# Identity products around the slot marks, own rows stored after the first gather, expert rows on ScalarE, value tiles of the last tile made at the start

## The chip, the cores and the metric

The kernel runs on one core of a Trainium2 chip, in one launch. The time is the device time of that launch in microseconds (us); a smaller time is better. Of the kernel before there are three timed runs and one execution that the hardware profiler recorded.

## The reference, cut to what matters

64 images are cut into 36 patches, and each image becomes 37 rows of 192 numbers (`h`, 64 x 37 rows). Then four blocks each add to `h`: causal linear attention, a soft mixture of 64 experts, and the two that this change touches: neighborhood attention, in which each row looks at a window of 5 images by 5 rows, and a mixture of 8 experts with two experts per row.

```
# neighborhood attention (k = 5, 4 heads)
xs = gelu(convB(convA(fc1(x))) + fc1(x))
q, kmat, vmat = xs @ qkv_w.T + qkv_b
sh = clip(arange(H) - 2, 0, H - 5)          # the window is clipped at both ends
attn = softmax(q . kmat[window] + rpb)
h = h + (attn . vmat[window]) @ proj_w.T @ fc2_w.T + ...
# routed experts (E = 8, two per row, CAP = 740 places each)
logits = xf @ gate_w.T
top_p, top_i = top_k(softmax(logits), 2)
pos = place of the row among those of its expert (cumulative count)
keep = pos < cap
buf = rows put into [expert, place]
z = 2 * buf; z = z * rsqrt(mean(z * z) + 1e-6) * norm_w
g, u = split(z @ w13)
y = buf + (silu(g) * u) @ w2
out = sum over the row's two places of weight * y
```

## The kernel before

**Tiles.** The rows of three images stand in one tile of 111 partitions (`TP`), and `T` = 22 such tiles hold all of `h`, in SBUF. Each engine has its own program, written out by hand; semaphores join them. A stage is a list of steps with lags that `over_tiles` unrolls: in turn s the step with lag k works on tile s - k, in the order of the list. The first turns and the last are written out, those between are a loop.

**Neighborhood attention** (`near_pe`, `near_dve`, `near_act2`, `near_pool`). After a first part that makes the keys, TensorE does in each turn: the query of a tile (`query`, L1587), one value tile (`value`, L1593), the scores of four heads (`scores`, L1611), the projection (L1647), the transposes of the weights (L1621 and L1622), the fc2 product (L1652), and the weights times the values (L1637). POOL copies the source columns of each value tile (L1335), normalizes the softmax weights (`normalize_w`, L1346) and adds a bias to the rows (L1352), in this order within its turn. VectorE (DVE) stores values (L1431), spreads the query over heads (L1427), adds the bias to the scores and takes their maximum (L1454), copies transposed weights (L1470) and adds the result to `h` (L1477), with statistics behind it (L1479). ScalarE (ACT) takes the exponentials (L1490) and copies (L1498, L1499, L1506, L1512, L1515).

The query and the value product write the same PSUM bank 0, so `spread` waits for the value product of its turn too. A tile uses three value tiles, which `vn` holds in a ring of four. The window is clipped at the end, so the last tile (t = 21) needs three value tiles of its own, `vl`; they have the numbers 23, 24 and 25 and are made in turn 24, in a chain POOL copy, TensorE product, DVE store, each waiting for the one before.

**Routing** (`route_dve`, `route_pe`, `route_act`). DVE makes statistics, the logits and the two best experts of each row. TensorE makes the counts before each row (two products, L1668 and L1669). DVE turns them into places, and makes marks for two tiles at a time (`marks`, L1800 to L1804, 11 pairs); for each pair TensorE does four products (`slots`, L1678) that add up, for every place of every expert, the row that stands there and its weight. Meanwhile POOL makes the normalized rows `zk` (L1842, 22 instructions), SP stores them to `z_rows` in DRAM (L1874), and when the place table `take` is ready, POOL gathers the rows of expert 0 and 1 (L1852, six indirect DMAs for each expert). DVE makes `own`, the row's own part of the output, and SP stores it to the output (L1879, L1884, L1885) as soon as it is ready; POOL waits for these seven stores before its first adding store (L1865).

**Experts** (`routed_pe`): transposes of the gathered rows (L1903, L1911), gate and up products (L1929, L1934), output products (L1943), for 8 experts.

`dense_near`, which stood in the kernel before, issues products whose result nobody reads:

```
for _ in range(times):
    nc.tensor.matmul(bank[5][:, 0:256], ident, cc[:, 0:256], start=True, stop=True)
```

Of the kernel before, what the change touches and what calls it, by code (L numbers as in the profile page):

```python
# [9 lines left out]
ACT = mybir.ActivationFunctionType  # L10
# [109 lines left out]
def tower(nc, ins, rows_out):  # L120
    with ExitStack() as ctx:
# [206 lines left out]
        zs = sb("zs", [TP, T])  # L328
        rlg = sb("rlg", [TP, T, EX])
# [945 lines left out]
        def value_columns(j):  # L1275

            return j * TP if not isinstance(j, int) or j <= T else (B - WIN + PADR) * S + (j - T - 1) * TP

        def value_tiles(t):

            if isinstance(t, int):
                return [T + 1, T + 2, T + 3] if t == T - 1 else [t + 2]
            return [t + 2]
# [19 lines left out]
        def near_pool(pool):  # L1303
# [33 lines left out]
            def sources(t, q):  # L1337

                source.b = q % 2
                for j in value_tiles(t):  # L1340
                    source(j)
# [20 lines left out]
            for j in range(2):  # L1362
                source(j)
# [23 lines left out]
        def near_dve(dve):  # L1387
# [31 lines left out]
            def spread(t, q):  # L1419
# [3 lines left out]
                if after(t, 3):  # L1423
                    dve.wait_ge(s_fV, t)
# [8 lines left out]
            def values(t, q):  # L1433
                if after(t, 2):
                    dve.wait_ge(s_nA, t - 1)
                for i, j in enumerate(value_tiles(t)):
                    value(j, vl[i] if isinstance(t, int) and t == T - 1 else vn[(q + 2) % 4])
# [43 lines left out]
            over_tiles(dve, [(4, copy_w), (2, reciprocal), (1, logits), (3, values), (0, spread), (5, residual)], T, unroll=4, tail=2)  # L1481
# [40 lines left out]
        def near_pe(pe):  # L1522
# [57 lines left out]
            def query(t, q):  # L1580
                if after(t, 1):
                    pe.wait_ge(s_nq, t)
                if after(t, 4):
                    pe.wait_ge(s_fVc, t - 1)
                elif t == 0:
                    pe.wait_ge(s_fVc, 2)
                nc.tensor.matmul(bank[0][0:WN, 0:TP], Cc["wq"], xg[:, bass.ds(PADR * S + t * TP, TP)], start=True, stop=True).then_inc(s_nQ, 1)  # L1587

# [6 lines left out]
            def values(t, q):  # L1595
# [3 lines left out]
                for j in value_tiles(t):  # L1599
                    value(j, (j if isinstance(j, int) else q) % 2)  # L1600
# [24 lines left out]
            def values_out(t, q):  # L1625
# [4 lines left out]
                pe.wait_ge(s_fVc, VT if isinstance(t, int) and t == T - 1 else t + 3)  # L1630
# [27 lines left out]
        def route_act(act):  # L1658
            h_std(act, 3)
            act.wait_ge(s_ph, 9 + 2)  # L1660
            nc.scalar.activation(zrt[:], zsq[:], ACT.Sqrt, bias=eps6[:], scale=4.0).then_inc(s_hsd, 1)
            act.wait_ge(s_rt, 1)
            nc.scalar.activation(wexp[:], wdif[:], ACT.Exp).then_inc(s_re, 1)

        def route_pe(pe):
# [4 lines left out]

            def slots(p, b):

                pe.wait_ge(s_oh, p + 1)
# [6 lines left out]

            over_tiles(pe, [(0, slots)], T // 2, tail=1)

        def route_dve(dve):
# [30 lines left out]
            nc.vector.scalar_tensor_tensor(out=zs[:], in0=zs[:], scalar=2.0, in1=hrs[:], op0=ALU.mult, op1=ALU.mult).then_inc(s_ph, 1)  # L1714
# [473 lines left out]
```

## Time and profile before

| | us |
|---|---|
| three timed runs | 961.99, 970.0, 974.12 (median 970.0) |
| profiled execution | 967.93 |
| its span, first to last instruction | 965.4 |
| TensorE busy | 839.8 (87%) |
| VectorE busy | 443.0 (46%) |
| ScalarE busy | 317.8 (33%) |
| POOL busy | 306.0 (32%) |
| mean granted TensorE clock | 0.92 of full |

The span is 2.5 us shorter than the time of the same execution. A busy share is an average over stages that differ: in the experts' stage TensorE is never idle, in the routing it is idle most of the time. So the stage tells what a change in it is worth. The granted clock has two levels, 1.0 (2.4 GHz) and 0.5 (1.2 GHz), and a stretch with a figure between had both.

### The profile page before, as it was taken

What the parts mean: (1) busy time and instruction counts of PE and PEld (TensorE: products, weight loads), DVE (VectorE), ACT (ScalarE), POOL (GpSimd) and SP (SyncE); (2) the same over time, 40 slices, a digit from 0 to 9 for tenths busy, and PEclk for the clock granted to TensorE, in tenths of its full rate; (3) what the DMA queues carried; (4) which work ended last, traced back from release to release, by engine and by line L of the source; (5) the groups of instructions that cost most, each with busy time, mean ns of one, the idle gap of its engine ahead of it and who ended that gap; (6) DMA issues with size and microseconds to landing.
All of it is one profiled execution on the core that took longest, in us unless ns stands there. A gap on an engine that the chain in (4) does not pass through costs nothing.

```text
span 965.4 us, 17426 instructions
## 1 busy us (share of the span) xinstructions
PE 839.8 (87%) x6089; PEld 601.3 (62%) x6089; DVE 443.0 (46%) x1486; ACT 317.8 (33%) x906; POOL 306.0 (32%) x267
## 2 busy tenths in 40 slices
PE   6889999899999999884898899994357999999991
PEld 6778888676556665543864577773344666666661
DVE  5764655558633322222635478863871222222220
ACT  2543333226533332223033377762001212122110
POOL 1440000000000000000125254541947588888444
PEclk9999999999989999997899599996556999999996
DMA  8994000090059999995130000000224355544222
GB/s 249 259 297 187 1 2 1 1 391 2 2 204 422 421 420 421 421 380 147 43 137 0 1 2 1 0 2 1 57 78 116 81 106 105 105 93 103 39 25 24
DMA packets 59881, 129.03 MB, mean 134 GB/s; under 512 B 26334, under 2 KB 42256, under 8 KB 50112
## 3 DMA queue, kind: packets, MB, share of 16 engines
q1 hardware_dynamic: 29858, 118.72, 34.2%
q0 software_dynamic: 29952, 9.36, 7.1%
q8 instruction: 44, 0.72, 0.3%
q14 instruction: 27, 0.22, 0.1%
HBM read 115.87 MB, written 11.49 MB: 132 GB/s over the span
## 4 chain that ended last, share of the span: by engine, by line
PE 72%; DMA 12%; DVE 5%; issue 4%; ACT 2%; SPq 2%; POOL 2%; DVEq 0%; POOLq 0%; ACTq 0%
PE bank L1929 9%; PE bank L1943 6%; PE bank L1934 5%; PE bank L1213 4%; DMA w1l<-in_w_dram 4%; PE bank L1611 3%; DMA xT<-in_xT_dram 3%; PE bank L1187 3%; PE bank L849 3%; PE bank L877 3%; DMA w1s<-in_w_dram 2%; PE bank L810 2%; PE bank L1637 2%; PE bank L1191 2%; PE bank L857 2%
## 5 line engine op out<-in xcount | busy, mean ns | idle before, releaser
L1305 POOL MEMSET xg<- 96x74 f32 x1 | 0.2, 158 | 405.9 <-PE bank L1269 405.9
L1865 POOL DMA_INDIRECT out_dram<-yr,put x48 | 105.8, 2203 | 58.2 <-issue 46.8
L1929 PE MATMUL bank<-zTa,w 128*128 128x372 f32 x256 | 90.3, 497 | 0.8 <-DVE zTb L2003 0.8
L2012 DVE TENSOR_TENSOR hT<-sg,bank 128x372 f32<-128x372 f32 x64 | 31.8, 538 | 107.7 <-ACT sg L1973 66.3
L1852 POOL DMA_INDIRECT zr<-z_rows,take x48 | 66.7, 1389 | 27.1 <-issue 26.8
L1929 PEld LDWEIGHTS bank<-zTa,w 128*128 128x128 f32 x256 | 47.5, 194 | 38.2 <-ACT sg L1973 8.4
L1153 DVE COPY eh<-bank 128x384 f32<-128x384 f32 x32 | 17.9, 558 | 111.5 <-PE bank L1191 111.5
L1943 PE MATMUL bank<-w2r,hT 128*124 128x192 f32 x384 | 66.1, 329 | 0.8 <-DVE hT L2012 0.8
L1973 ACT ACTIVATE sg<-bank 128x372 f32<-128x372 f32 x64 | 27.3, 478 | 115.6 <-PE bank L1934 115.6
L1943 PEld LDWEIGHTS bank<-w2r,hT 128*124 128x124 f32 x384 | 61.9, 187 | 3.9 <-issue 3.9
L1346 POOL TENSOR_TENSOR nl<-nl,nr 111x1036 f32<-111x1036 f32 x22 | 42.1, 1914 | 60.3 <-DVE nr L1463 60.3
L1490 ACT ACTIVATE nl<-nl,nn 111x259 f32<-111x259 f32 x88 | 43.9, 501 | 40.0 <-DVE nn L1456 40.0
L1611 PE MATMUL bank<-kT,qx 96*111 (+1 forms) x176 | 52.7, 429 | 1.4 <-DVE nm L1454 1.4
L810 PE MATMUL bank<-wtok_c,xT 128*111 128x192 f32 x264 | 46.7, 331 | 8.1 <-DMA xT<-in_xT_dram 5.1
L810 PEld LDWEIGHTS bank<-wtok_c,xT 128*111 128x111 f32 x264 | 42.0, 176 | 12.8 <-issue 6.4
L1934 PE MATMUL bank<-zTb,w 64*128 64x372 f32 x256 | 48.7, 498 | 0.0
L1454 DVE CUSTOM_DVE_ANT_0 nl<-bank,bias 111x259 f32<-111x259 f32 x88 | 36.6, 424 | 15.4 <-issue 15.1
L1213 PE MATMUL bank<-w2l,eg 128*64 128x192 f32 x480 | 43.4, 330 | 0.0
L1121 ACT ACTIVATE eg<-eg 128x768 f32<-128x768 f32 x32 | 27.1, 846 | 40.6 <-DVE eg L1164 40.6
L1116 ACT COPY eh<-bank 128x384 f32<-128x384 f32 x32 | 15.4, 480 | 70.2 <-PE bank L1191 70.2
L1934 PEld LDWEIGHTS bank<-zTb,w 64*128 64x128 f32 x256 | 22.0, 186 | 24.8 <-issue 17.2
L1213 PEld LDWEIGHTS bank<-w2l,eg 128*64 128x64 f32 x480 | 32.7, 137 | 7.1 <-issue 3.3
(311 smaller groups left out, 1757.8 us busy)
## 6 DMA issues: line engine op xcount, KB each, us to landing
w1l<-in_w_dram SPq DMA_DIRECT2D x20, 1152.0 KB, 16.0
w2l<-in_w_dram SPq DMA_DIRECT2D x20, 1152.0 KB, 16.8
w1s<-in_w_dram SPq DMA_DIRECT2D x12, 1152.0 KB, 14.9
w2s<-in_w_dram SPq DMA_DIRECT2D x12, 1152.0 KB, 15.0
w<-in_w_dram SPq DMA_DIRECT2D x8, 1024.0 KB, 7.8
xt<-in_x_dram SPq DMA_DIRECT2D x22, 336.0 KB, 8.9
xT<-in_xT_dram SPq DMA_DIRECT2D x22, 333.0 KB, 8.1
w2r<-in_w2r_dram SPq DMA_DIRECT2D x8, 384.0 KB, 4.0
```

Of the source, the lines that this page charges most:

```text
L810: last = nc.tensor.matmul(bank[2 + q % 2][0:TP, 0:ED], xT[q][:, k, :], wtok_c[:, k, :], start=(k == 0), stop=(k == KC - 1))
L1213: last = nc.tensor.matmul(bank[6 + b][e * B:(e + 1) * B, 0:ED], eg[b][:, j, e, :], w2s[q][:, e, j, :], start=(j == 0), stop=(j == HB - 1))
L1346: nc.gpsimd.tensor_tensor(nl[q][:], nl[q][:], nr[b][:].unsqueeze(2).to_broadcast([TP, NHN, KW]), ALU.mult).then_inc(s_nw, 1)
L1454: nc.vector.tensor_tensor_reduce(nl[q][:, head, :], bank[1 + head % 2][0:TP, 0:KW], bias[v][:, head, :], 1.0, -3.0e38, ALU.add, ALU.max, n ...
L1490: last = nc.scalar.activation(nl[q][:, head, :], nl[q][:, head, :], ACT.Exp, bias=nn[b][:, head:head + 1], accum_out=nsum[b][:, head:head ...
L1611: nc.tensor.matmul(bank[1 + head % 2][0:TP, 0:KW], qx[q % 2][:, head, :], kT[:, bass.ds(first, KW)], start=True, stop=True).then_inc(s_nS, 1)
L1852: nc.gpsimd.indirect_dma_start(zr[b][:, j, :], None, z_rows, bass.IndirectOffsetOnAxis(ap=take[:, k:k + 1], axis=0), bounds_check=NROW - 1 ...
L1865: nc.gpsimd.indirect_dma_start(rows_out, bass.IndirectOffsetOnAxis(ap=put[:, k:k + 1], axis=0), yr[e % 2][:, j, :], None, bounds_check=OUT ...
L1929: nc.tensor.matmul(bank[to + 2 * part + half][:, 0:HS], w13[b][:, 0, at:at + 128], zTa[b][:, half * HS:(half + 1) * HS], start=True, stop= ...
L1934: nc.tensor.matmul(bank[to + 2 * part + half][:, 0:HS], w13[b][rows, 1, at:at + 128], zTb[b][rows, :], start=False, stop=True).then_inc(s_ ...
L1943: last = nc.tensor.matmul(bank[2 + j % 2][0:SP_, 0:ED], hT[:, m, j * SP_:(j + 1) * SP_], w2r[b][:, m, :], start=(m == 0), stop=(m == EH // ...
L2012: nc.vector.tensor_tensor(hT[:, m, half * HS:(half + 1) * HS], sg[half][:], bank[4 * (m % 2) + 2 + half][:, 0:HS], ALU.mult).then_inc(s_hT, 1)
```

## The change

Four edits. **Values**: the three value tiles of the last tile get the numbers 2, 3 and 4 and are made in the first three turns, each behind the query of its turn, with two identity products behind it; the ordinary value tiles move up by three numbers, and turn 24 has no value product and no POOL copy. **Identity products**: 14 after the two count products, 2 ahead of the wait of each `slots`, 22 after the last `slots`; all in bank 6. **Expert rows**: `zk` is made by ScalarE (22 activations with scale `zs` and bias `zb`, which one new DVE instruction makes) ahead of the exponential of the routing weights, and no more by POOL. **Own rows**: SP waits until the first gather (`s_zr[0]`) has landed before it stores own rows.

```
@@ value_columns, value_tiles
-            return j * TP if not isinstance(j, int) or j <= T else (B - WIN + PADR) * S + (j - T - 1) * TP
+            if isinstance(j, int) and j < 2:
+                return j * TP
+            if isinstance(j, int) and j < 5:
+                return (B - WIN + PADR) * S + (j - 2) * TP
+            return (j - 3) * TP
-            if isinstance(t, int):
-                return [T + 1, T + 2, T + 3] if t == T - 1 else [t + 2]
-            return [t + 2]
+            return [] if isinstance(t, int) and t == T - 1 else [t + 5]
@@ near_pool
-            for j in range(2):
+            for j in range(5):
                 source(j)
@@ near_dve
                 dve.wait_ge(s_nQ, t + 1)
-                if after(t, 3):
-                    dve.wait_ge(s_fV, t)
+                dve.wait_ge(s_fV, t + 3)
...
+            def last_values(t, q):
+                if isinstance(t, int) and t < 3:
+                    value(t + 2, vl[t])
...
-            over_tiles(dve, [(4, copy_w), (2, reciprocal), (1, logits), (3, values), (0, spread), (5, residual)], T, unroll=4, tail=2)
+            over_tiles(dve, [(4, copy_w), (2, reciprocal), (1, logits), (3, values), (0, spread), (0, last_values), (5, residual)], T, unroll=4, tail=2)
@@ near_pe
-                if after(t, 4):
-                    pe.wait_ge(s_fVc, t - 1)
-                elif t == 0:
-                    pe.wait_ge(s_fVc, 2)
+                pe.wait_ge(s_fVc, t + 2)
                 nc.tensor.matmul(bank[0][0:WN, 0:TP], Cc["wq"], xg[:, bass.ds(PADR * S + t * TP, TP)], start=True, stop=True).then_inc(s_nQ, 1)
+                if isinstance(t, int) and t < 3:
+                    value(t + 2, t % 2)
+                    dense_near(2)
@@ route_act
             nc.scalar.activation(zrt[:], zsq[:], ACT.Sqrt, bias=eps6[:], scale=4.0).then_inc(s_hsd, 1)
+            act.wait_ge(s_ph, 9 + 5)
+            for t in range(T):
+                nc.scalar.activation(zk[:, t, :], h[:, t, :], ACT.Identity, bias=zb[:, t:t + 1], scale=zs[:, t:t + 1]).then_inc(s_gz, 1)
             act.wait_ge(s_rt, 1)
@@ route_pe
+            def dense_route(times, to):
+                for _ in range(times):
+                    nc.tensor.matmul(bank[to][:, 0:256], ident, cc[:, 0:256], start=True, stop=True)
             def slots(p, b):
+                dense_route(2, 6)
                 pe.wait_ge(s_oh, p + 1)
...
+            dense_route(14, 6)
             over_tiles(pe, [(0, slots)], T // 2, tail=1)
+            dense_route(22, 6)
@@ route_dve
+            dve.wait_ge(s_ph, 9 + 4)
+            nc.vector.scalar_tensor_tensor(out=zb[:], in0=hmean[:], scalar=-1.0, in1=zs[:], op0=ALU.mult, op1=ALU.mult).then_inc(s_ph, 1)
@@ rows_pool
-            pool.wait_ge(s_ph, 9 + 4)
-            for t in range(T):
-                nc.gpsimd.tensor_scalar(zk[:, t, :], h[:, t, :], hmean[:, t:t + 1], zs[:, t:t + 1], ALU.subtract, ALU.mult).then_inc(s_gz, 1)
@@ routed_sp
             out_of = rows_out[0:NROW].rearrange("(t p) d -> p t d", p=TP)
+            sp.wait_ge(s_zr[0], 16 * SJ)
```

On POOL at the end of the neighborhood attention (turn 24 and behind it) stood three source copies, then the normalization of tile 21 and the bias additions:

```order
L1346 TENSOR_TENSOR nl0<-nl0,nr0 111x1036
L1352 TENSOR_TENSOR h21<-h,cc 111x192
L1335 COPY vsrc1<-xg 96x111
L1335 COPY vsrc0<-xg 96x111
L1335 COPY vsrc1<-xg 96x111
L1346 TENSOR_TENSOR nl1<-nl1,nr1 111x1036
L1352 TENSOR_TENSOR h20<-h,cc 111x192
```

The copies are gone there, and the normalization follows at once:

```order
L1338 COPY vsrc1<-xg 96x111
L1349 TENSOR_TENSOR nl0<-nl0,nr0 111x1036
L1355 TENSOR_TENSOR h21<-h,cc 111x192
L1349 TENSOR_TENSOR nl1<-nl1,nr1 111x1036
L1355 TENSOR_TENSOR h20<-h,cc 111x192
```

On TensorE at the start of the turns (`vsrc` the source of a value tile, `qx` the spread query) stood two value products, two queries, then the scores of tile 0:

```order
L1593 MATMUL bank0<-cc,vsrc0 111x96
L1593 MATMUL bank0<-cc,vsrc1 111x96
L1587 MATMUL bank0<-xg,cc 96x111 x2
L1611 MATMUL bank1<-kT,qx0 111x259
L1611 MATMUL bank2<-kT,qx0 111x259
```

Now a value product and two identity products stand behind each of the first three queries, so four identity products and two value products are ahead of the first scores:

```order
L1599 MATMUL bank0<-cc,vsrc1 111x96
L1590 MATMUL bank0<-xg,cc 96x111
L1599 MATMUL bank0<-cc,vsrc0 111x96
L1534 MATMUL bank5<-cc,identity 128x256 x2
L1590 MATMUL bank0<-xg,cc 96x111
L1599 MATMUL bank0<-cc,vsrc1 111x96
L1534 MATMUL bank5<-cc,identity 128x256 x2
L1617 MATMUL bank1<-kT,qx0 111x259
```

On TensorE in the routing stood the two count products and then the slot products of each pair (`ohc`, `ohp` the marks):

```order
L1668 MATMUL bank2<-hots,cc 111x176
L1669 MATMUL bank3<-hots,ones 111x176
L1678 MATMUL bank4<-ohc0,ohp0 124x96 x4
L1678 MATMUL bank4<-ohc1,ohp1 124x96 x4
L105 UNCONDITIONAL_BRANCH
```

Now 16 identity products (14 and the first pair's 2) lie between, two more ahead of each later pair:

```order
L1677 MATMUL bank2<-hots,cc 111x176
L1678 MATMUL bank3<-hots,ones 111x176
L1682 MATMUL bank6<-cc,identity 128x256 x16
L1692 MATMUL bank4<-ohc0,ohp0 124x96 x4
L1682 MATMUL bank6<-cc,identity 128x256 x2
L1692 MATMUL bank4<-ohc1,ohp1 124x96 x4
```

## Rows read from the trace of the kernel before

**Rows 1.** Stretches: us, busy PE, PEld, DVE, ACT, POOL, then granted clock, DMA share, GB/s
```profile
526.00:540.00 14.00, 9.96 (x34) 6.82 (x34) 4.55 (x19) 3.29 (x9) 0.77 (x3) 0.54 0.00 1
652.00:657.00 5.00, 0.61 (x10) 0.44 (x4) 1.40 (x4) 1.37 (x4) 3.65 (x5) 0.98 0.00 0
657.00:671.00 14.00, 10.78 (x76) 6.91 (x76) 3.18 (x9) 4.24 (x10) 0.52 (x1) 0.50 0.00 1
692.00:713.00 21.00, 19.79 (x88) 18.42 (x88) 15.85 (x45) 0.00 (x0) 9.55 (x7) 0.50 0.21 57
```
**Rows 2.** Timeline, last turns: start, us, engine, line, operation, [idle before <-releaser]
```profile
648.48 0.18 DVE L1463 RECIPROCAL nr<-nsum 111x4 f32<-111x4 f32 x1
...
652.75 0.52 ACT L1499 COPY pTb<-bank 37x444 f32<-37x444 f32 x1
652.78 1.91 POOL L1346 TENSOR_TENSOR nl<-nl,nr 111x1036 f32<-111x1036 f32 x1
...
656.87 0.66 PE L1593 MATMUL bank<-cc,vsrc 96*111 96x96 f32 x2 [4.39 <-DVE vl L1431]
...
658.79 0.58 PE L1621 MATMUL bank<-identity,nl 111*111 111x111 f32 x2
...
669.18 1.03 PE L1652 MATMUL bank<-cc,nz 104*111 104x208 f32 x2 [0.44 <-ACT nz L1515]
```
**Rows 3.** Timeline: queries and first scores of the first turns, and a later query
```profile
532.23 0.69 PE L1587 MATMUL bank<-xg,cc 96*96 96x111 f32 x2 [0.35 <-DVE vn L1431]
...
534.16 3.73 PE L1611 MATMUL bank<-kT,qx 96*111 96x259 f32 x8
...
539.21 0.69 PE L1587 MATMUL bank<-xg,cc 96*96 96x111 f32 x2 [1.31 <-DVE qx L1427]
...
551.34 0.36 PE L1587 MATMUL bank<-xg,cc 96*96 96x111 f32 x2
...
556.20 0.43 PE L1587 MATMUL bank<-xg,cc 96*96 96x111 f32 x2
```
**Rows 4.** Timeline: products at the full clock and at half
```profile
500.86 1.56 PE L1528 MATMUL bank<-cc,identity 128*128 128x256 f32 x6
733.82 5.18 PE L1929 MATMUL bank<-zTa,w 128*128 128x372 f32 x8 [0.80 <-DVE zTb L2003]
740.38 2.77 PE L1929 MATMUL bank<-zTa,w 128*128 128x372 f32 x8
```
**Rows 5.** Timeline: routing, from the counts to the first marks
```profile
675.57 25.98 POOL L1842 TENSOR_SCALAR zk<-h,hmean,zs 111x192 f32<-111x192 f32 x22 [12.64 <-DVE zs L1714]
675.74 0.52 DVE L1726 TENSOR_TENSOR eq<-rlg,top 111x176 f32<-111x176 f32 x1
678.27 0.33 DVE L1726 TENSOR_TENSOR eq<-lg,top 111x176 f32<-111x176 f32 x1
689.02 0.17 DVE L1784 TENSOR_SCALAR wsum<-wexp 111x22 f32<-111x22 f32 x1
691.77 3.62 PE L1678 MATMUL bank<-ohc,ohp 111*124 111x96 f32 x16 [9.58 <-DVE ohc L1804]
```
**Rows 6.** Chain of work that ended last, from the slots to expert 0
```profile
723.05 6.88 DMA zr<-z_rows,take
729.97 1.50 PE bank L1903 x6
```
**Rows 7.** Timeline: SP's stores of own rows, and POOL's first adding store
```profile
718.05 6.10 SPq L1879 DMA_DIRECT2D out_dram<-h x4
...
728.38 2.20 SPq L1885 DMA_DIRECT2D out_dram<-h x1
...
756.71 2.26 POOL L1865 DMA_INDIRECT out_dram<-yr,put x1 [12.02 <-issue]
```
**Rows 8.** The gathered rows zr: time from issue to landing, 48 transfers
```profile
DMA to landing us min/median/max: 3.9/4.3/7.2
```
**Rows 9.** Groups by line and form: an activation with a scale for each partition
```profile
L633 ACT ACTIVATE yn<-y,yrs 111x192 f32<-111x192 f32 x22 | 9.6, 441 | 0.0
```

More of the change, by code:

```diff
@@ L328, in tower @@
         zs = sb("zs", [TP, T])
+        zb = sb("zb", [TP, T])
         rlg = sb("rlg", [TP, T, EX])
@@ L1337, in sources @@
             def sources(t, q):
-                source.b = q % 2
+                source.b = (q + 1) % 2
                 for j in value_tiles(t):
@@ L1435, in values @@
                     dve.wait_ge(s_nA, t - 1)
-                for i, j in enumerate(value_tiles(t)):
-                    value(j, vl[i] if isinstance(t, int) and t == T - 1 else vn[(q + 2) % 4])
+                for j in value_tiles(t):
+                    value(j, vn[(q + 2) % 4])
+            def last_values(t, q):
+                if isinstance(t, int) and t < 3:
+                    value(t + 2, vl[t])
             for j in range(2):
@@ L1599, in values @@
                 for j in value_tiles(t):
-                    value(j, (j if isinstance(j, int) else q) % 2)
+                    value(j, (q + 1) % 2)
             for j in range(2):
@@ L1629, in values_out @@
                 tiles = vl if isinstance(t, int) and t == T - 1 else [vn[(q + i) % 4] for i in range(3)]
-                pe.wait_ge(s_fVc, VT if isinstance(t, int) and t == T - 1 else t + 3)
+                pe.wait_ge(s_fVc, VT if isinstance(t, int) and t == T - 1 else t + 6)
                 if after(t, 1):
```

## The prediction

> **What bounds the kernel now.** I read the busy time by stretch first, then the timeline and the chain that ended last where a stretch looks poor. Up to the first turns of the neighborhood attention and from expert 0's products on, nothing is changed, so only some 200 us between can move. In them TensorE runs long at the lower clock, 0.50: in most of 526 to 540, in all of 657 to 671 and of 692 to 713 [rows 1]. Three waits stand out.
>
> The first is at the end of the neighborhood attention. From 652.5 to 656.9 TensorE does nothing and its clock has gone to 0.50 when it goes on [rows 1, 2]. The weights of tile 21 could be normalized from 648.66 on, when the reciprocal is done, but POOL begins at 652.78 [rows 2], since the source copies of the last tile's values stand ahead of it and each waits for a product on TensorE. POOL's bias additions come after, DVE's residual waits for these, and DVE's stores of values stand behind the residual, so TensorE waits for them.
>
> The second is the routing: TensorE is idle for 9.6 us ahead of the first slot product, and then does the 44 slot products at half clock, 0.45 us each (3.62 us for 8) [rows 5], with DVE waiting for it in turn.
>
> The third is the gather. The sixth indirect DMA of expert 0 is issued at 723.05 and lands 6.88 us later, at 729.97, when the transposes start [rows 6]; the least of the 48 is 3.9 and the median 4.3 us [rows 8]. SP's stores of own rows, 718.05 to 730.6, lie beside it [rows 7].
>
> **Last turns.** Without the three copies the normalization starts at 648.7 and ends at 650.6, and nothing late is left ahead of the bias additions. The next to be late is ScalarE's copy of transposed weights, which ends at 653.27; the transposes of tile 21 can start at 653.35 instead of 658.79 [rows 2]: 5.4 us. From there to the end of the last fc2 product at 670.21 it was 11.4 us. I estimate that hand-offs over ScalarE take 4.2 of it and TensorE 7.2, at half clock. If the clock stays high this is halved, 3.6 us less, as the gate products took 5.18 us at half and 2.77 at the full clock [rows 4]. So the bounds are -5.4 (clock falls at once) and -9.0 (it stays). The stall that had let it fall is gone, but these turns have no scores and TensorE will still wait a microsecond at each hand-off. I take -8.0.
>
> **First turns.** The three value products are now here, with six identity products. The identity products at full clock: 6 records, 3 products, in 1.56 us with the last one's latency, so 0.47 us each from start to start; at half clock I scale by columns from the gate product, 5.18 us for 4 products of 372 columns [rows 4], to 0.86 us. The first scores began at 534.16 [rows 3]. Now ahead of them, from 532.23 on at half clock: query and value product (1.0), two identity products (1.7), again both (2.7), so they begin at about 537.9, 3.7 us late. Against that TensorE now works without a gap from 532.2 on, and the clock should rise in or before these scores instead of in the turn before 551.34. Scores that took 3.73 us then take about 2.5, and a turn from query to query 4.9 (551.34 to 556.20), where the two turns from 539.21 to 551.34 took 6.1 each [rows 3]. Laid out: scores from 537.9 to 540.4, then 0.9 for DVE's last maximum and spread as before (537.9 to 539.2 with its wait), third query at 541.3 (was 539.21); then two turns of 4.9, the first with 0.9 of identity products, so the fifth query at 551.9 (was 551.34). That is +0.5. Bounds: -1.5 if the clock rises at once, +4.5 if not before the third turn. The later turns have the same order and the same waits as before, with other numbers.
>
> **ScalarE's rows.** The nearest row is an activation of 111x192 with a scale for each partition, 0.441 us [rows 9]; 22 of them are 9.7 us, from about 675.8 to 685.5. Behind them stands the exponential of the routing weights, with a table load of some 1.3 us, so it is done at about 687; DVE reads it at 689.02 [rows 5]. That cover is 2 us; without it each microsecond would be paid. SP stores `zk` long before the gathers. DVE has one more instruction with a semaphore wait ahead of the first maximum: +0.2. POOL's 25.98 us go away [rows 5], and they were hidden; but the same comparison on DVE took 0.52 us as POOL's first one began and 0.33 later, also beside POOL [rows 5]. I take -0.4 for all of DVE's chain.
>
> **Routing.** The count products end at 682.2, 9.58 us before the first slot product at 691.77 [rows 5]. The 14 identity products are 12.0 us if the clock stays at half. The first gate products, from 733.82 on without a pause, took 5.18 us for eight records, those from 740.38 on 2.77 [rows 4]: the clock rose after some 5 us of unbroken work. With 5 us at half (6 products) and 8 at 0.47, they end at 691.0, and the pair of the first slots at 691.9: +0.2. Then a pair of tiles costs 2 x 0.47 of identity products and 4 x 0.24 of slot products (0.45 scaled by 2.77/5.18), 1.9 us, against 1.81 before (3.62 / 2). DVE's marks are shorter: it is busy for 15.85 of the 21 us [rows 1], about 1.5 a pair, so TensorE sets the pace. The first four products and ten such pairs are 19.9 us; before it was 20.4 (691.77 to the end of the 44th at 712.2, of which 0.5 in waits). With the +0.2 I take -0.3. The higher clock is spent on the products that keep it. Bounds -2.5 (identity products hidden better) and +2.
>
> **Gather.** `take` is ready, and POOL issues, at the same distance from the last slot product. Without SP's stores beside them the rows land in 3.9 to 4.3 us instead of 6.88 [rows 6, 8]: -2.8, bounds 0 and -3.0. The stores took 12.5 us before [rows 7]; begun at 727 they end at about 740 on the scale of the trace before. POOL waits for them ahead of its gather for expert 2, 10 us of issue, and the first adding store, at 756.71 before [rows 7], would be due some 3 us earlier: hidden with 3 us to spare. Later stores would delay the first adding stores, which only expert 2's output buffers wait for.
>
> **First expert.** The 22 identity products last 10.4 us, the wait from the last slot product to the landed rows about 15. The idle 4.7 us are as long as the 4.4 us after which the clock was at half [rows 1, 2]. So the gate products start cold, as before: 0. If the clock were kept, the first 5.18 us would be 2.77, the transposes 1.3 us less: -3.9 in all [rows 4].
>
> **Sum.** -8.0 + 0.5 + 0.2 - 0.4 - 0.3 - 2.8 = -10.8. Against the profiled execution's own 967.9 (span 965.4 and 2.5 around it) that is 957.1. This execution was 2 us below the median of 970.0, which itself has runs from 962 to 974; I forecast 957.
>
> **Rivals.**
> A, the forecast, clock as above: 957, chance 0.47, own range 951 to 962.
> B, the clock is kept throughout: -9.0 in the last turns, -1.5 in the first, -2.5 in the routing, -3.0 for the gather, -3.9 for the first expert, -0.2 for DVE; -20.1 together, 948. For it: in rows from 740 on the clock stays high. Against it: the idle 4.7 us. Chance 0.20.
> C, the first turns lose and the last ones run cold: -5.4 + 4.5 - 0.2 + 0 - 2.8 = -4, 964. For it: from 534 to 551 TensorE was busy most of the time and stayed at half, with waits for DVE of 1.3 us [rows 3]. Or the stores were not what delayed the gather (that term at 0): 960. Chance 0.23.
> D, slower: the identity products don't raise the clock in the routing. For it: 692 to 713 had TensorE busy for 19.79 of 21 us, still at 0.50 [rows 1]. Then a pair costs 1.7 + 1.8 us; 14 products make the first slots 4 us late, ten pairs with 1.7 more each 17 more, and the 22 end 18.9 us after the last slot, 3.7 us after the rows. 4 + 17 + 3.7 - 2.8 = 22; with -8.0 for the last turns, +0.5 for the first and -0.2 for DVE's chain +14, 982. It decides once the clock is still low after the fourth pair, since 4 + 4 x 1.7 then eat up the 10.5 won elsewhere. Against it: the gate products, issued without a wait, raised the clock [rows 4], and the 14 identity products come without a wait too. Chance 0.05.
> E, POOL had held DVE up throughout: if each of its instructions in front of 691.77, 14 of the 22, cost DVE the 0.19 us between the two comparisons [rows 5], 2.6 us go instead of 0.4: 955. Against it: the second comparison also ran beside POOL, unhindered. Chance 0.05. The Trainium skill, "SBUF — State Buffer", section "Who interferes with whom", has a DVE instruction with two SBUF inputs and a GpSimd instruction that reads SBUF exclude each other for a whole instruction, which speaks for E; the row of the second comparison does not show it.
> That the change doesn't do what it says would be to have POOL's normalization still late; the order excludes it.
>
> **Range and chances.** A with its range, E, C up to 964 and a part of B hold 8 in 10 between 948 and 965. Faster by over 2% (below 950.7 against the median, 948.5 against the profiled time) is most of B and a little of A: 0.17. Slower by over 2% is a worse D: 0.02. Within 2%, about what a measurement of this kernel can tell from no change, the rest, 0.81.
>
> **What would show it.** Right: no idle time of over 1.5 us on TensorE between the loop's end and the last fc2 product, statistics some 8 us earlier; granted clock near 1.0 among the slot products; a landing of about 4 us; half clock in the first gate products. Wrong: a third query later than 543, DVE waiting for ScalarE's exponential, slots at 0.50, POOL waiting for own rows ahead of its first adding store.

## The result, and the profile after

The changed kernel takes 955.3 us (median of 20 runs, 951.2 to 963.2), the kernel before 968.0 us in the same series (20 runs, 962.0 to 974.1). The ratio is 0.989, with a 95% interval of 0.9867 to 0.9913: about 10.7 us less (8.4 to 12.9 by the interval; the two medians are 12.7 apart). So the gain is clear of the noise and under 2%. The profiled execution of the changed kernel has a span of 949.4 us, the one of before 965.4. One run of this study, of 958.8 us in f1 below, is over 1.5% above the fastest run of its kernel and counts as slow, and f1's figures leave it out.

Of these 16.0 us, 5.1 are not the change's. They lie ahead of the first query of the neighborhood attention, in code that no edit touches: the first query starts at 532.23 us before and at 527.14 after, and in the fourteen profiled executions of this study it starts anywhere from 523.9 to 537.0. So everything below is counted from the first query on. From there to the end it is 433.2 us before and 422.3 after, 10.9 less, which agrees with the ratio. (f0, the same kernel in another execution, has 423.0, 10.2 less.)

The table cuts this stretch at rows that every kernel here has, and gives each piece in us. "Marks" is the slot stage, from the first slot product to the moment when VectorE, which waits for the last one, reads the sums. "All" is their sum, and "time" that of the whole profiled execution, which has the varying part ahead of the first query in it too. "To counts" ends where the first count product starts, "to transposes" where the first product on the gathered rows of expert 0 starts. f0 is the changed kernel profiled once more. Each row is one execution, and where kernels have the same code a stage can still differ: the last turns by 1.5 us (23.63 to 25.18), the stage to the end by 1.7 (234.35 to 236.08 with 22 identity products ahead of it).

| | first to sixth query | to last query | to last fc2 product's end | to counts | to first slot product | marks | to transposes | to the end | all | time |
|---|---|---|---|---|---|---|---|---|---|---|
| before | 23.97 | 81.43 | 32.58 | 10.46 | 11.10 | 20.44 | 17.76 | 235.43 | 433.2 | 967.9 |
| after | 25.74 | 82.03 | 25.17 | 10.36 | 10.01 | 18.49 | 14.96 | 235.50 | 422.3 | 951.2 |
| e1 | 24.06 | 81.40 | 32.58 | 10.35 | 10.00 | 18.49 | 15.01 | 235.15 | 427.0 | 960.4 |
| e2 | 26.29 | 82.03 | 23.92 | 10.34 | 10.34 | 18.39 | 14.93 | 236.08 | 422.3 | 948.0 |
| e3 | 25.34 | 82.03 | 23.75 | 10.36 | 10.56 | 18.39 | 17.97 | 234.37 | 422.8 | 954.7 |
| e4 | 25.38 | 82.02 | 23.75 | 10.34 | 10.58 | 18.39 | 14.87 | 232.08 | 417.4 | 947.1 |
| e5 | 25.42 | 82.02 | 23.63 | 10.44 | 11.08 | 18.49 | 14.96 | 235.65 | 421.7 | 956.7 |
| e6 | 25.37 | 82.02 | 23.69 | 10.36 | 10.01 | 20.15 | 15.09 | 235.40 | 422.1 | 960.9 |
| e7 | 25.01 | 82.03 | 23.93 | 10.36 | 10.01 | 18.33 | 15.13 | 235.89 | 420.7 | 954.2 |
| e8 | 25.80 | 82.03 | 25.18 | 10.36 | 10.89 | 27.02 | 14.91 | 234.35 | 430.5 | 967.6 |
| f0 | 27.54 | 82.02 | 23.91 | 10.36 | 10.13 | 18.39 | 15.06 | 235.60 | 423.0 | 953.9 |
| f1 | 28.02 | 82.03 | 23.92 | 10.35 | 10.01 | 15.08 | 14.99 | 233.57 | 418.0 | 949.6 |
| f2 | 24.26 | 82.03 | 23.68 | 10.34 | 11.58 | 14.98 | 14.87 | 231.66 | 413.4 | 950.3 |
| g1 | 23.64 | 82.02 | 23.69 | 10.35 | 9.35 | 15.09 | 15.05 | 233.71 | 412.9 | 944.7 |

The first view of after is the busy time by stretch, with the columns of [rows 1]: us, busy PE, PEld, DVE, ACT, POOL, then granted clock, DMA share, GB/s.

```profile
649.00:654.00 5.00, 3.78 (x54) 2.57 (x50) 2.09 (x5) 2.42 (x8) 1.05 (x2) 1.00 0.01 3
654.00:661.00 7.00, 4.21 (x31) 2.06 (x30) 1.52 (x5) 3.17 (x7) 0.00 (x0) 0.56 0.00 0
671.00:681.00 10.00, 10.00 (x41) 8.47 (x40) 8.31 (x35) 5.83 (x12) 0.00 (x0) 0.78 0.61 166
681.00:700.00 19.00, 19.00 (x132) 17.82 (x131) 15.03 (x46) 0.00 (x0) 0.00 (x0) 1.00 0.00 1
714.00:718.00 4.00, 3.16 (x19) 2.41 (x20) 1.21 (x2) 1.85 (x2) 3.26 (x3) 0.50 0.79 209
```

The marks, at 0.50 before [rows 1], now run at 1.00 (681 to 700). The last turns begin at 1.00 and end at about half; expert 0 still starts at 0.50 (714 to 718).

The timeline of TensorE over the last turns (start, us, engine, line, operation, idle before and releaser) answers to [rows 2]:

```profile
650.65 0.42 PE L1627 MATMUL bank<-identity,nl 111*111 111x111 f32 x2 [0.44 <-issue]
...
655.10 1.03 PE L1658 MATMUL bank<-cc,nz 104*111 104x208 f32 x2 [1.07 <-ACT nz L1521]
...
659.05 1.03 PE L1658 MATMUL bank<-cc,nz 104*111 104x208 f32 x2 [0.44 <-ACT nz L1521]
```

The stop of 4.39 us is gone; the longest wait left is 1.07 us. Behind it an fc2 product takes 1.03 us where it took 0.52 a turn earlier: there the clock fell.

The same view over the routing, to set beside [rows 5], then the gather:

```profile
670.44 0.93 PE L1677 MATMUL bank<-hots,cc 111*111 111x176 f32 x2 [10.35 <-DVE hots L1760]
...
671.74 8.85 PE L1682 MATMUL bank<-cc,identity 128*128 128x256 f32 x32
680.45 1.11 PE L1692 MATMUL bank<-ohc,ohp 111*124 111x96 f32 x8
681.39 1.06 PE L1682 MATMUL bank<-cc,identity 128*128 128x256 f32 x4
...
683.12 1.05 PE L1682 MATMUL bank<-cc,identity 128*128 128x256 f32 x4
...
698.74 9.69 PE L1682 MATMUL bank<-cc,identity 128*128 128x256 f32 x44
713.90 1.50 PE L1918 MATMUL bank<-identity,zr 124*128 124x124 f32 x6 [5.47 <-DMA zr<-z_rows,take]
```

A product is two records, so the slot products of a pair are x8. From 681.39 to 683.12 a pair and its two identity products take 1.73 us. And the chain of work that ended last, at the gather, beside [rows 6]:

```profile
708.07 1.38 POOL zr L1866
709.75 4.10 DMA zr<-z_rows,take
713.90 1.50 PE bank L1918 x6
```

The rows that held the kernel up land 4.10 us after their issue, not 6.88.

### The profile page after: what moved, and what is told of

It reads as the page before. It is cut to its first block, busy times and chain, and to the rows that moved or that the text cites. A ratio compares the mean times of both kernels' runs of the same rounds, so it can differ in the third digit from the quotient of the medians.

```text
span 949.4 us, 17704 instructions
## 1 busy us (share of the span) xinstructions
PE 849.1 (89%) x6217; PEld 612.3 (64%) x6217; DVE 441.2 (46%) x1487; ACT 327.1 (34%) x928; POOL 279.8 (29%) x245
## 4 chain that ended last, share of the span: by engine, by line
PE 73%; DMA 12%; issue 4%; DVE 3%; SPq 3%; ACT 2%; POOL 1%; DVEq 0%; POOLq 0%; ACTq 0%
PE bank L1944 9%; PE bank L1958 6%; PE bank L1949 5%; DMA w1s<-in_w_dram 4%; PE bank L1617 4%; PE bank L1214 4%; PE bank L850 3%; PE bank L1188 3%; PE bank L811 3%; PE bank L878 3%; DMA xT<-in_xT_dram 3%; DMA w2l<-eo 2%; DMA w1l<-in_w_dram 2%; PE bank L1682 2%; PE bank L1627 2%
## 5 line engine op out<-in xcount | busy, mean ns | idle before, releaser
L1617 PE MATMUL bank<-kT,qx 96*111 (+1 forms) x176 | 49.6, 406 | 2.2 <-DVE nm L1460 2.0
```

The source lines that it names most:

```text
L1617: nc.tensor.matmul(bank[1 + head % 2][0:TP, 0:KW], qx[q % 2][:, head, :], kT[:, bass.ds(first, KW)], start=True, stop=True).then_inc(s_nS, 1)
```

## The experiments

Each experiment is the changed kernel with the edit shown. e1 to e8 were each executed once, with a profile; f0, f1, f2 and g1 were also timed six times, in rounds with the kernel before. The table above has the stages of all of them.

**e1: value tiles of the last tile late again.** Numbering, rings and waits of the value tiles as in the kernel before, and so none of the six identity products of the first turns either; the other three edits stay. One piece of the edit:

```
-            return [] if isinstance(t, int) and t == T - 1 else [t + 5]
+            if isinstance(t, int):
+                return [T + 1, T + 2, T + 3] if t == T - 1 else [t + 2]
+            return [t + 2]
```

> The changed kernel with the last tile's three value tiles back in turn 24, without the identity products of the first turns; the routing as changed. In the trace of the changed kernel the stretch from the last query to the end of the last fc2 product is 25.2 us, in that of before 32.6. Theory (POOL's source copies hold back the normalization of tile 21, and the clock falls in the stall): it is 32 to 33 us again, and the stretch from the first query to the sixth is 24.0 again, not 25.7; in all 5 to 6 us slower than the changed kernel. Rival (part of the 7.4 us came from the clock's phase in that one execution): 27 to 30 us.

The last turns take 32.58 us again, to a hundredth what they took before, and the first ones 24.06. So the edit is worth -7.4 there in the profiled execution of after and costs +1.7 in the first turns. In all e1 is 4.7 us slower than after, where 5 to 6 were expected. The loop between takes 81.40 with the old numbering and 82.0 with the new one, in every kernel: 0.6 us that the prediction did not have. POOL's timeline of e1 has the mechanism as the prediction named it:

```profile
647.83 0.28 POOL L1336 COPY vsrc<-xg 96x111 f32<-96x111 f32 x1 [2.15 <-PE bank L1594]
651.94 0.28 POOL L1336 COPY vsrc<-xg 96x111 f32<-96x111 f32 x1 [3.83 <-PE bank L1594]
652.18 1.91 POOL L1347 TENSOR_TENSOR nl<-nl,nr 111x1036 f32<-111x1036 f32 x1
```

The normalization (L1347) follows the third copy, which waits 3.83 us for TensorE.

**e2: no identity products in the first turns.**

```
                     value(t + 2, t % 2)
-                    dense_near(2)
```

> The changed kernel without the six identity products of the first three turns; the value tiles stay there. Theory of the prediction (the products cost 3.5 us ahead of the first scores and give it back by an earlier clock): first query to first scores 2 to 2.5 us instead of 5.0, first to sixth query 24 to 26 us, within 1 us of the changed kernel's 25.7. Rival (they only cost): under 23 us, since the waits of DVE set the pace of these turns. Rival 2 (they pay): over 27 us, half clock up to the sixth query.

26.29 us to the sixth query: 0.3 above what the theory allowed, far from the first rival (under 23) and below the second (over 27), so none of the three is met. The first scores come 2.92 us after the first query and run at half clock (3.76 us for eight records), as the next two groups do. Kernels that have the products there in the changed kernel's form were profiled nine times: seven of them need 25.0 to 25.8, two (f0 and f1) 27.5 and 28.0. So the value tiles alone cost 2.3 us, and beside this one profile the six identity products give back 0.5 to 1.3 or lose 1.2 to 1.7; with one profile without them, what they are worth on the whole is not settled. What sets which it is, the timelines of TensorE show. After:

```profile
530.45 1.81 PE L1534 MATMUL bank<-cc,identity 128*128 128x256 f32 x4
532.11 1.04 PE L1617 MATMUL bank<-kT,qx 96*111 96x259 f32 x4
...
536.00 0.40 PE L1590 MATMUL bank<-xg,cc 96*96 96x111 f32 x2 [1.58 <-DVE vl L1433]
...
541.25 0.41 PE L1590 MATMUL bank<-xg,cc 96*96 96x111 f32 x2 [1.61 <-DVE vl L1433]
...
541.67 3.58 PE L1617 MATMUL bank<-kT,qx 96*111 96x259 f32 x8
```

and f0, the same kernel:

```profile
532.50 1.97 PE L1534 MATMUL bank<-cc,identity 128*128 128x256 f32 x4
534.26 1.32 PE L1617 MATMUL bank<-kT,qx 96*111 96x259 f32 x4
...
538.45 0.66 PE L1590 MATMUL bank<-xg,cc 96*96 96x111 f32 x2 [1.58 <-DVE vl L1433]
...
545.26 0.66 PE L1590 MATMUL bank<-xg,cc 96*96 96x111 f32 x2 [1.60 <-DVE vl L1433]
```

In both the clock rises near the end of the identity products. In f0 it is some tenths later (1.97 and 1.32 us against 1.81 and 1.04), and after the first wait of 1.58 us for VectorE it is at half again (a query takes 0.66 us, not 0.40); in after it falls only behind the second such wait. The turns with the waits then take 6.8 and 6.7 us, or 5.25 and 6.0.

**e3: own rows stored at once**, ahead of the gather, as before.

```
             out_of = rows_out[0:NROW].rearrange("(t p) d -> p t d", p=TP)
-            sp.wait_ge(s_zr[0], 16 * SJ)
```

> The changed kernel with SP storing own rows at once, beside the first gather. Theory (SP's stores delay the gathered rows): the sixth transfer of expert 0 lands 6.5 to 7 us after its issue instead of 4.1, the first transposes start 17.5 to 17.8 us after the last slot product instead of 15.0; 2.5 to 3 us slower. Rival (the landing of 6.88 was a matter of that execution, or came with POOL's earlier work): 15 us and no change.

The wait for the rows is 17.97 us instead of 14.96. The other stages differ from after's by up to 1.4 us in both directions, but each stays within what the kernels without this edit show. In e3's chain the landing stands as

```profile
711.38 7.10 DMA zr<-z_rows,take
```

So the stores beside it were what delayed it, by 3.0 us (a landing of 6.5 to 7 us had been expected).

**e4: 34 identity products behind the marks** instead of 22.

```
-            dense_route(22, 6)
+            dense_route(34, 6)
```

> The changed kernel with 34 identity products behind the last slot product instead of 22, so that they last until the rows of expert 0 land. In the changed kernel TensorE is idle for 5.5 us there, the clock is at half in the transposes and the first gate products. Theory (these 5.5 us let the clock fall; the 22 products give nothing): from the landing to the second group of gate products 6.7 us instead of 10.6, so 3.5 to 4 us faster. Rival (transposes and their hand-offs let the clock fall anyway): 9 to 10.6 us, no change.

Its timeline of TensorE:

```profile
698.05 14.87 PE L1682 MATMUL bank<-cc,identity 128*128 128x256 f32 x68
713.12 0.85 PE L1918 MATMUL bank<-identity,zr 124*128 124x124 f32 x6 [0.20 <-DMA zr<-z_rows,take]
714.32 0.85 PE L1926 MATMUL bank<-identity,zr 124*64 124x124 f32 x12 [0.34 <-ACT zTa L1980]
715.98 2.74 PE L1944 MATMUL bank<-zTa,w 128*128 128x372 f32 x8 [0.80 <-DVE zTb L2018]
```

The transposes take 0.85 instead of 1.50 us, the first gate products 2.74 instead of 5.30: from the landing to the end of these gate products 3.6 us less, and from the transposes to the end of the kernel 3.4. The changed kernel stops its identity products 5.47 us too early for this. Both figures depend on the execution, for with 22 products the first gate products take anything from 4.17 (e8) to 5.30 us; beside e8 the gain would be 2.3 us.

**e5: expert rows on POOL again.**

```
-            act.wait_ge(s_ph, 9 + 5)
-            for t in range(T):
-                nc.scalar.activation(zk[:, t, :], h[:, t, :], ACT.Identity, bias=zb[:, t:t + 1], scale=zs[:, t:t + 1]).then_inc(s_gz, 1)
+            pool.wait_ge(s_ph, 9 + 4)
+            for t in range(T):
+                nc.gpsimd.tensor_scalar(zk[:, t, :], h[:, t, :], hmean[:, t:t + 1], zs[:, t:t + 1], ALU.subtract, ALU.mult).then_inc(s_gz, 1)
```

> The changed kernel with the 22 normalized expert rows made by POOL again, after DVE's scale, and no bias instruction. In the changed kernel the stretch from the end of the last fc2 product to the first slot product is 20.4 to 20.9 us, in that of before 21.6; and the slot stage 18.4 to 18.5 us. Theory E of the prediction (POOL's instructions hold up DVE): 21.4 to 21.7 us, and the first pairs of marks slower. Rival (the 1.2 us came from something else, such as the clock or the counts): 20.4 to 20.9 us.

From the counts to the first slot product 11.08 us, where the changed kernel has 10.01 and the kernel before has 11.10. That stretch is VectorE's here: TensorE has done its identity products and waits 0.28 us for the marks. From the end of the count products it is 9.57 us in e5 and 9.58 before, with POOL's instructions, and 8.50 in after, e6 and g1, without them. The marks behind it take 18.49 us as in after: the slower first pairs that the theory added did not come. VectorE's timeline in e5, with POOL beside it:

```profile
669.80 0.52 DVE L1739 TENSOR_TENSOR eq<-rlg,top 111x176 f32<-111x176 f32 x1
...
676.64 0.34 DVE L1768 COPY sums<-sums 111x8 f32<-111x8 f32 x1
```

and in the changed kernel:

```profile
665.83 0.34 DVE L1744 TENSOR_TENSOR eq<-rlg,top 111x176 f32<-111x176 f32 x1
...
672.36 0.17 DVE L1773 COPY sums<-sums 111x8 f32<-111x8 f32 x1
```

POOL's instructions of 1.18 us each (25.98 / 22 [rows 5]) cost VectorE 0.1 to 0.25 us now and then, most often in the short copies behind the counts, and add up to 1.1 us. The Trainium skill, "SBUF — State Buffer", section "Who interferes with whom", names a VectorE instruction with two SBUF inputs and, in the 2-port modes, a copy as those that contend with GpSimd, and says of the port pair that they share: "Whoever issues first gets the shared pair for the whole instruction". The rows agree that they interfere (the comparison has two SBUF inputs), and not on the size: no instruction of VectorE was held up by anything like POOL's 1.18 us.

**e6: no identity products in the routing at all** (neither the 14, nor the 2 per pair, nor the 22).

> The changed kernel without any identity product in the routing (the 14, the 2 in each pair, the 22). Theory (the slot products without them run at half clock, 0.45 us each, 1.81 us a pair, and TensorE sets the pace): the slot stage 20.2 to 20.5 us instead of 18.4; nothing else moves, so 2 us slower. Rival (the slot stage became shorter since POOL no longer works beside DVE): 18.4 to 19 us.

The marks take 20.15 us, as they did before (20.44). The busy time by stretch:

```profile
688.00:699.00 11.00, 10.48 (x48) 10.00 (x48) 8.84 (x25) 0.00 (x0) 0.00 (x0) 0.50 0.00 0
699.00:708.00 9.00, 8.96 (x41) 8.34 (x40) 6.29 (x18) 0.00 (x0) 0.00 (x0) 0.50 0.00 0
```

TensorE is busy for 19.44 of 20 us and stays at 0.50. All 58 identity products of the routing together are worth 1.7 us. The counts to the first slot product are 10.01 us here as in after: VectorE sets that stretch, and in after the 14 products just fit into it. They don't always. In e2, e3, e4 and f0 TensorE goes from the identity products to the slot products without a gap, and the first slot product comes after 10.13 to 10.58 us (10.89 in e8, with two more ahead of it): where the clock rises late, the products hold it up by 0.1 to 0.6 us.

**e7 and e8: none, or four, ahead of each pair** instead of two; the 14 and the 22 stay.

> The changed kernel with the 14 and the 22 identity products, but none between the pairs of slot products. Theory 1 (the clock that the 14 raised stays up, since TensorE then waits for DVE's marks only a part of each pair): pairs at DVE's pace of 1.65 us, the stage 17 to 17.6 us instead of 18.4, so the two in each pair cost 1 us. Theory 2 (the waits for DVE let the clock fall in the stage): 19.5 to 20.5 us.

> The changed kernel with four identity products ahead of each pair instead of two. Theory (TensorE sets the pace of the slot stage, and a pair costs what its products cost at the full clock): two more at 0.44 us each, a pair 2.62 instead of 1.74 us, the stage 27 to 28 us instead of 18.4. Rival (DVE's marks set the pace): under 20 us.

e7 needs 18.33 us for the marks, as with two: between the two theories (17 to 17.6, and 19.5 to 20.5), since the pace that the first had for VectorE was too slow and the fall of the clock, which the second has, came late. Its timeline and its stretches:

```profile
683.05 1.11 PE L1691 MATMUL bank<-ohc,ohp 111*124 111x96 f32 x8 [0.42 <-DVE ohc L1821]
...
688.64 12.71 PE L1691 MATMUL bank<-ohc,ohp 111*124 111x96 f32 x56 [0.29 <-DVE ohc L1821]
```

```profile
682.00:689.00 7.00, 5.42 (x37) 4.33 (x37) 7.00 (x21) 0.00 (x0) 0.00 (x0) 0.98 0.00 0
689.00:699.00 10.00, 9.94 (x47) 9.46 (x47) 8.07 (x23) 0.00 (x0) 0.00 (x0) 0.50 0.00 0
```

For five pairs VectorE sets the pace, 1.40 us a pair (four from 683.05 to 688.64), and TensorE waits 0.29 us in each. Then the clock falls, TensorE sets the pace at half clock, 1.8 us a pair, and never gets it back. With two identity products (after) the clock stays, but they cost TensorE 0.89 us a pair, so 1.73 is what a pair takes. The two come out even. With four, a pair takes 2.60 us (690.36 to 692.96) and the stage 27.02:

```profile
690.36 1.92 PE L1682 MATMUL bank<-cc,identity 128*128 128x256 f32 x8
692.12 1.01 PE L1692 MATMUL bank<-ohc,ohp 111*124 111x96 f32 x8
692.96 1.92 PE L1682 MATMUL bank<-cc,identity 128*128 128x256 f32 x8
```

That pointed to one: 0.44 + 0.84 = 1.28 us for TensorE, less than VectorE's 1.40, with 0.12 to wait instead of 0.29.

**f0, f1, f2: the changed kernel, one ahead of each pair, and more in other places.** f1 has one identity product per pair and 34 behind the marks. f2 adds to f1:

```
@@ query
+                if isinstance(t, int) and t in (2, 3):
+                    dense_near(3)
@@ fc2 of the last two tiles (dense_last: the same product in bank 2)
+                if isinstance(t, int) and t >= NLT:
+                    dense_last(2)
@@ route_pe, ahead of the counts and behind them
+            for _ in range(12):
+                nc.tensor.matmul(bank[2][:, 0:256], ident, cc[:, 0:256], start=True, stop=True)
...
-            dense_route(14, 6)
+            dense_route(18, 6)
```

> The changed kernel once more, so that f1 and f2 have it beside them on the same chip. Nothing is altered. From the two executions timed side by side so far: 0.989 of the kernel before, interval about 0.985 to 0.993, so 955 to 958 us beside 967. Stages as in its first profile: last query to last fc2 product 23.8 to 25.2 us, counts to first slot product 10.0 to 10.6, slot stage 18.4 to 18.5, gather 15.0.

> The changed kernel with one identity product instead of two ahead of each pair of marks, and 34 instead of 22 behind the last slot product. Theory (the identity products are worth what the clock they keep gives back, and no more of them is wanted than keeps it): a pair of slots then costs TensorE 0.44 + 0.84 = 1.28 us, less than VectorE's 1.40, so VectorE sets the pace and the slot stage takes 15 to 16 us instead of 18.4, at granted clock 1.00; behind it the 34 products keep the clock up to the transposes, 3.4 us less as in e4. Together 6 to 7 us less than the changed kernel, some 949 to 951 where that has 956. Rival: with 0.12 us of waiting in each pair the clock falls among the slots, as it did with none in e7, and the stage stays at 18 to 19 us; then only e4's 3.4 us are left, some 952 to 953.

> f1 with identity products in three more places where TensorE waits at half clock: three ahead of the third and fourth query of the first turns, two ahead of each fc2 product of the last two tiles, twelve ahead of the count products and 18 instead of 14 behind them. Theory (a waiting TensorE loses its clock, and products nobody reads keep it at no cost while it would wait anyway): first to sixth query 1 us less than the 25.7 of the changed kernel, last query to last fc2 product 23.2 to 23.8 us in each execution, last fc2 product to first slot product up to 1 us less; 1 to 2.5 us less than f1. Rival: each stands ahead of a product that is wanted, and delays it by its own 0.44 us (0.86 at half clock), so what the clock gives is spent: no difference from f1, or up to 2 us more.

Medians: f0 955.5 us, ratio to the kernel before 0.9893 (0.9854 to 0.9932). f1 949.6 us (five runs), 0.9826 (0.9769 to 0.9882). f2 949.9 us, 0.9811 (0.9771 to 0.9852). f1's timeline:

```profile
684.16 1.11 PE L1692 MATMUL bank<-ohc,ohp 111*124 111x96 f32 x8
...
685.56 1.09 PE L1692 MATMUL bank<-ohc,ohp 111*124 111x96 f32 x8
...
717.08 4.43 PE L1944 MATMUL bank<-zTa,w 128*128 128x372 f32 x8 [0.80 <-DVE zTb L2018]
```

A pair takes 1.40 us (684.16 to 685.56) and the marks 15.08 us, 3.3 less, as the theory had it. The gain behind the marks is 2.0 us instead of 3.4: the transposes were at the full clock, but in the first gate products it fell (4.43 us, where e4 has 2.74). Together 5 us by the stages, and 5.9 by the medians of f0 and f1, where 6 to 7 were expected.

f2's first turns take 24.26 us: the three identity products lie in the waits for VectorE that undid the clock. The last turns take 23.68, inside the expected range; without the extra products eight executions have 23.6 to 23.9. But from the counts to the first slot product it is 11.58 us. The twelve products ended 5.16 us ahead of the counts, the clock was low again for these, and eighteen products are then more than VectorE's 10 us cover. By the stages of one execution each f2 is 4.6 us ahead of f1 (1.9 of them behind the transposes, where the two kernels have the same code); by the medians it is level with it (949.9 and 949.6). Runs that spread over 8 us for f2 and 14 for f1 cannot tell these, so that f2's products gain 1 to 2.5 us is not shown.

**g1: f2 with 22 products ahead of the counts.**

> f2 with 22 instead of 12 identity products ahead of the count products. In f2 the twelve ended 5.2 us before the counts, the counts ran at half clock again, and with 18 products behind them the first slot product came 11.6 us after the counts where the changed kernel has 10.0 (VectorE's time for places and marks, which e6 with no products there has too). Theory: 22 products at the full clock are 9.7 of the 10.35 us from the last fc2 product to the counts; the clock is then still high, the two count products take 1.0 instead of 1.5 us, the 18 products behind them 7.9 us, and VectorE sets the pace again: 9.3 to 9.7 us from counts to first slot product, 1.9 to 2.3 us less than f2, so about 948 beside 950. Rival: the clock has fallen in the 0.6 us of waiting, and the 18 products take 11 us or more again: no change from f2.

The median is 948.8 us, the ratio 0.9815 (0.9768 to 0.9862).

```profile
659.18 9.66 PE L1684 MATMUL bank<-cc,identity 128*128 128x256 f32 x44
669.70 0.55 PE L1687 MATMUL bank<-hots,cc 111*111 111x176 f32 x2 [0.86 <-DVE hots L1770]
670.09 0.46 PE L1688 MATMUL bank<-hots,ones 111*111 111x176 f32 x2
670.39 8.37 PE L1692 MATMUL bank<-cc,identity 128*128 128x256 f32 x38
679.05 1.11 PE L1702 MATMUL bank<-ohc,ohp 111*124 111x96 f32 x8 [0.29 <-DVE ohc L1832]
```

The clock lasts over the 0.86 us of waiting, the counts take 0.55 and 0.46 us instead of 0.93 and 0.79, and the first slot product comes 9.35 us after them: 2.2 less than in f2, 0.7 less than in the changed kernel. By the stages g1 has 20.3 us less than the kernel before, the changed kernel 10.9; measured, 18.7 (967.5 to 948.8) and 12.7 (968.0 to 955.3). It has the lowest median of this study, some 7 us below the changed kernel, but it cannot be told from f2 (ratios 0.9815 and 0.9811): the 2.2 us are seen in the one execution's stage, and not in the time of the kernel. Its interval ends where that of the changed kernel in the long series begins (0.9867), and overlaps the one of f0.

## Why the prediction came true, step by step

The forecast was 957 us, from a sum of -10.8. The stages give -10.9 and the medians 955.3. But several terms were off, in both directions, and cancelled: the first turns, the loop and the last turns cost 2.5 us more than forecast in the profiled execution, the routing up to the last mark 2.6 less (-1.2 and -1.95, where -0.5 had been taken in all). That the sum came out to 0.1 is luck, and f0's stages, with other misses, give -10.2. The total does not tell A from E either, which said 955; e5 does.

- **Last turns, -8.0.** -7.4 in the profiled execution. In the ten profiles with this code, the same stage takes 25.2 us twice and 23.6 to 23.9 eight times, so some -8.8 mostly, near the bound of -9.0. The removed copies are the cause (e1).
- **First turns, +0.5.** +1.8, and +3.6 and +4.0 in f0 and f1, near the bound of +4.5. (The forecast was laid out to the fifth query only, where it is +1.0 in after.) Up to the third query the layout held: 8.86 us after the first where 9.1 had been laid out. (The terms named there, 1.0 + 1.7 + 2.7, give first scores 5.4 us after the first query and not the 5.7 written; they came after 4.97.) The step that failed is the one after it, "two turns of 4.9": the clock rose as said, but TensorE then waits 1.6 us twice for VectorE's store of `vl`, and falls to half in the next turn. That the query now waits for a store that stands behind VectorE's maximum and spread is in the diff, and I had reckoned its length and not what it does to the clock. f2 and g1 put work into these waits, and the cost is gone.
- **Loop, nothing.** +0.6, in every kernel with the new numbers and not in e1, which has the old. The turns between the queries are 5.0 to 5.2 us in both, but at one of the loop's returns a turn takes 5.52 instead of 5.12 and at the next 5.22 instead of 5.09. "The same order and the same waits as before, with other numbers" was not enough to call it nothing. Why the return costs more was not tried.
- **VectorE's extra instruction +0.2, freed of POOL -0.4, first slots +0.2.** Together -1.2 from the last fc2 product to the first slot product, not 0. The term of POOL was sized from one comparison, and e5 gives it as 1.1. Rival E was right in kind, wrong in size and place: not 14 hindrances of 0.19 each, but a few of 0.1 to 0.2, most of them behind the counts. And the 14 products are hidden in VectorE's work in after (e6), while they reach past it by 0.1 to 0.6 us in four other executions, as the +0.2 had it.
- **Marks, -0.5 (19.9 from 20.4).** -1.95. The pace was TensorE's, as said, but each product was mis-sized: a slot product at the full clock takes 0.21 us (0.84 for four) and not the 0.24 scaled from the gate products, an identity product 0.44 and not 0.47. So a pair takes 1.73 and not 1.9 us, and ten pairs 1.7 less.
- **Gather, -2.8.** -2.80, and e3 undoes it alone.
- **First expert, 0.** +0.1 in after: at half clock, behind 5.47 us of idle time. e4 gives the -3.9 of the other case as -3.4.
- **ScalarE's rows.** 22 activations in 9.74 us, as the 9.7 worked out. The exponential stands at 676.64 and VectorE reads it at 677.92, so its cover was 1.1 us instead of the 2 named. POOL does wait for the own rows ahead of its first adding store, which was named as a sign of error, but it does so ahead of the gather for expert 2, and the stage behind is as long as before (235.5 us):

```profile
729.27 1.38 POOL L1866 DMA_INDIRECT zr<-z_rows,take  x1 [8.03 <-DMA out_dram<-h]
```

**The rivals.** B (clock kept throughout) did not come. g1, with more products, has its 948 us, but by another sum: the marks give 5.4 us there instead of a part of 2.5, and the first gate products still lost the clock (4.43 us, as in f1). D (clock not raised among the marks) did not come: sixteen identity products without a wait raised it, and e6 shows that the marks alone do not. C came in its first half, in f0 and f1.

## What to carry to other kernels

Products that nobody reads are worth what the clock they keep gives back to the products behind them, less what they delay. All 58 in the routing of this change gave 1.7 us, and the 36 of e7 gave the same marks. Put them where TensorE would wait anyway, enough to reach the end of the wait; in a loop whose pace another engine sets, take the largest number that leaves TensorE faster than that engine (here one per pair, where none and two gave the same 18.4 us and one gave 15.1). And when work is moved to an earlier place, look at what the new wait there does to the clock, not only at its length.

## What the runs showed of the hardware

Slot products kept TensorE busy for 19.44 of 20 us at the granted clock 0.50 without raising it (e6), while unbroken identity products ahead of them raised it (after: 0.78 from 671 to 681, then 1.00). Once raised, it held through the marks with one or two identity products per pair, and fell after five pairs with none, where TensorE had been busy for 5.42 of 7 us (e7). With 34 identity products up to 0.2 to 0.4 us ahead of the landing, the transposes ran at the full clock in all four executions, and the first gate products behind them in two (2.74 us in e4 and f2, 4.43 in f1 and g1). The same program had its clock rise and fall at other moments from execution to execution: 4.9 us after the first query in after, 5.6 in f0. In the first turns these two differ by 1.8 us. Short copies of VectorE took 0.34 us beside POOL's work and 0.17 without it.
